# A decoder layer on one core: the last key blocks of two heads mixed together, and a few orders changed

## The reference

```python
x = x + attn(layernorm(x))                       # x: 2 x 512 x 1024
x = x + fake_quant(layernorm(x)) @ fake_quant(ctx)   # ctx: 2 x 1024 x 1024
x = x + experts(layernorm(x))
# attn: q = x@Wq (32 heads of 128), k = x@Wk and v = x@Wv (8 heads), rotary on q and k,
#   softmax(causal(q@k.T / sqrt(128))) @ v, each k and v head used by 4 q heads, then @ Wo (4096 x 1024)
# fake_quant: (clip(round(x/s + z), 0, 255) - z) * s
# experts: router of 64 experts, softmax over the top 16; z = x@A.T (512), gated by expert, @ B.T, times 2
```

## Time and profile before

| | |
|---|---|
| median of 3 runs | 1296.77 us (1296.71 to 1297.16) |
| the profiled execution | 1296.9 us, span 1295.1 us |
| mean granted clock of TensorE | 0.997 |
| TensorE busy | 1262.9 us of 6929 matmuls and transposes, 98% of the span |
| VectorE, ScalarE, GpSimd busy | 835.9 (65%), 767.2 (59%), 609.0 (47%) |
| one head unit with two jobs | about 10.3 us |
| transfers | mean 161 GB/s over the span |

### The profile page before, as it was taken

One profiled execution on the slowest core, in us unless ns is written; L12 is line 12 of the kernel. 1 busy time (PEld: TensorE's weight loads), 2 busy tenths in 40 slices (PEclk: granted clock), 3 DMA queues, 4 the chain that ended last, 5 costly groups with the idle time before them and its releaser, 6 DMA issues. The chain is left out here.

```text
span 1295.1 us, 19782 instructions
## 1 busy us (share of the span) xinstructions
PE 1262.9 (98%) x6929; PEld 1085.7 (84%) x6929; DVE 835.9 (65%) x1866; ACT 767.2 (59%) x1577; POOL 609.0 (47%) x450
## 2 busy tenths in 40 slices
PE   9999999999999999999999998999999999998998
PEld 8898998888888888888888887878888887766887
DVE  7774735556556656656556565655786788788763
ACT  4412247767777877777777877863333355565530
POOL 4777666779758777677766754420000000021100
PEclk9999999999999999999999999999999999999999
DMA  8033245558659568486485678758874486201111
GB/s 276 25 131 123 79 134 188 155 138 210 218 151 244 164 169 244 133 204 169 118 237 143 158 221 259 212 177 259 283 200 128 152 273 217 79 7 29 50 42 49
DMA packets 122403, 208.74 MB, mean 161 GB/s; under 512 B 15408, under 2 KB 56368, under 8 KB 118720
## 3 DMA queue, kind: packets, MB, share of 16 engines
q1 hardware_dynamic: 118272, 178.10, 42.5%
q0 software_dynamic: 4032, 29.36, 12.2%
HBM read 147.40 MB, written 88.08 MB: 182 GB/s over the span
## 5 line engine op out<-in xcount | busy, mean ns | idle before, releaser
L1253 DVE TENSOR_TENSOR pT_lo<-banks,pT_hi 128x512 fp32r<-128x512 f32 (+1 forms) x192 | 103.6, 595 | 170.7 <-ACT pT_hi L984 170.7
L1665 PE MATMUL banks<-ob_hi,oa_hi 128*128 128x512 f32 x384 | 149.5, 389 | 0.9 <-DVE ob_lo L1293 0.9
L1665 PE MATMUL banks<-ob_hi,oa_lo 128*128 128x512 f32 x384 | 149.4, 389 | 0.0
L1665 PE MATMUL banks<-ob_lo,oa_hi 128*128 128x512 f32 x384 | 149.4, 389 | 0.0
L1623 PE MATMUL banks<-xc,nring_hi_a 128*128 128x512 f32 x448 | 139.9, 393 | 2.1 <-DVE q_made L1203 2.1
L1623 PE MATMUL banks<-xc,nring_hi_b 128*128 128x512 f32 x448 | 139.5, 392 | 0.0
L968 ACT CAST oa_hi<-oraw 128x1024 fp32r<-128x1024 f32 x48 | 50.4, 1050 | 142.9 <-PE banks L1665 129.1
L984 ACT CAST pT_hi<-banks 128x512 fp32r<-128x512 f32 (+1 forms) x192 | 86.6, 527 | 66.0 <-PE banks L1593 66.0
L1879 POOL TENSOR_TENSOR resid<-resid,colterm 128x1024 f32<-128x1024 f32 x8 | 19.0, 2379 | 216.6 <-ACT colterm L1937 137.5
L737 POOL TENSOR_TENSOR q_lo<-q_raw,q_hi 128x512 fp32r<-128x512 f32 x64 | 87.0, 1360 | 38.5 <-ACT q_hi L921 38.2
L1578 PE MATMUL banks<-kT,q_hi 128*128 128x512 f32 (+2 forms) x384 | 104.2, 352 | 0.0
(11 more groups left out here) (256 smaller groups left out, 3413.8 us busy)
## 6 DMA issues: line engine op xcount, KB each, us to landing
q_raw<-qk_dram SPq DMA_DIRECT2D x64, 256.0 KB, 4.2
o_S<-o_st SPq DMA_DIRECT2D x64, 256.0 KB, 4.0
w<-in_L_attn_Wo SPq DMA_DIRECT2D x32, 512.0 KB, 5.9
oraw<-o_S SPq DMA_DIRECT2D x32, 512.0 KB, 3.7
nraw<-in_L_attn_Wq SPq DMA_DIRECT2D x28, 512.0 KB, 5.3
o_S<-o_S POOLq DMA_DIRECT2D x12, 1024.0 KB, 10.0
o_S<-o_N POOLq DMA_DIRECT2D x12, 1024.0 KB, 10.2
resid<-in_x SPq DMA_DIRECT2D x16, 512.0 KB, 7.1
```

The costliest lines, as they stand in the source:

```text
L1253: nc.vector.tensor_tensor(pT[1][:, sl], turned_chunk(turned, mixed, c), as32(pT[0][:, sl]), ALU.subtract).then_inc(pT_lo, 1)
L1665: ins = nc.tensor.matmul(step_bank(m, t), oa[a][:, s % 2, k, t * P:(t + 1) * P], ob[c][:, s % 2, k, :], start=(q == 0 and k == 0 and i == ...
```

## The change

1. The last key block (j = 3) of two neighbouring units, v = 2m and v + 1, is mixed together. Both have the same k and v head. `pT` grows from 1280 to 1408 columns: an even unit's transposed block 3 is put at column 512, an odd unit's at column 1024, so both are there when the odd unit is mixed. `mix` leaves block 3 out; in odd units three matmuls of 256 columns over both blocks go to `turned[:, 1, 0:256]` in bank 4.
2. VectorE adds them up (`add_pair`, three instructions): it copies the odd unit's 128 columns to SBUF and adds them to `mixed`, and adds the even unit's 128 columns, which stay in PSUM, to `o_st[0]` (subtracts them for batch 1). It runs after `normalise` of the next even unit, the last one after `step_low(0)`.
3. Those who wait for the addition (`pair_added`): ScalarE's `keep_out` of odd units, TensorE before the second chunk of the transposes of even units, and SyncE's `keep_out` of even units. SyncE now issues `keep_out(u - 3)` and `keep_out(u - 2)` together in its odd iterations. At the end `load_step(0)` and `load_step(1)` go ahead of the last two.
4. Memory: `identb` and `one` share their place with the copy of the odd block and are made by GpSimd after the last addition, not at the start; `small` shrinks, and the mask sum of tile 0 is kept in `prob`.
5. Start: 60 warm-up transposes instead of 72; the row statistics of tile 1 are made by ScalarE in five instructions (two passes over 1024 columns with sums).
6. Unit 57: the first half of step 1 (`first_high(1)`) on ScalarE goes behind the copies of the probabilities of unit 56, on GpSimd behind q's low part.
7. Last stretch: the loop's turn i = 1 is written out in another order. z of tile 0 goes before root(2) and scale_of(2), the b parts 6 and 7 before the reading of product 3, and the gate of tile 1 before product_stats(3), root(3) and scale_of(3).

```diff
-WARM = 72
+WARM = 60
-KEYS_AT = {0: 0, 1: 512, 3: 896, 2: 1024}
-CHUNKS = ((0, (0,)), (512, (1, 3)), (1024, (2,)))
+CHUNK_KEYS = ((0,), (1, 3), (2,))
+PT = 1408
+    def keys_at(u, j):
+        return {0: 0, 1: 640, 2: 1152, 3: 1024 if u % 2 else 512}[j]
+    def chunk_at(u, c):
+        return (0, 640 if u % 2 else 512, 1152)[c]
+    def last_blocks(part):
+        return pT[part][:].rearrange("p (k c) -> p k c", c=P)[:, 4:9:4, :]
...
         def keep_out(u):                                   # SyncE
             sp.wait_ge(o_copied, u + 1)
+            if u % 2 == 0:
+                sp.wait_ge(pair_added, u // 2 + 1)
...
-            if u >= 2:
+            if u >= 3 and u % 2:
+                keep_out(u - 3)
                 keep_out(u - 2)
...
-        keep_out(UNITS - 2)
         load_step(0)
         load_step(1)
+        keep_out(UNITS - 2)
         keep_out(UNITS - 1)
...
-            for f in steps_of(u + 1):                      # GpSimd
-                first_low(f)
-                if f == 0:
-                    turn_added(JOBS - 1)
+            if u == LAST_JOB_UNIT:
+                first_low(0)
+                turn_added(JOBS - 1)
+            elif u == LAST_JOB_UNIT + 1:
+                for f in range(1, 4):
+                    first_low(f)
+            else:
+                for f in steps_of(u + 1):
+                    first_low(f)
...
         def keep_out(u):                                   # ScalarE
             act.wait_ge(mix_done, u + 1)
+            if u % 2:
+                act.wait_ge(pair_added, u // 2 + 1)
             if u >= 2:
                 act.wait_ge(o_kept[u % 2], o_count(u - 2))
...
+            if u == LAST_JOB_UNIT + 1:                     # after probs_high
+                first_high(1)
...
+        def add_pair(u):                                   # VectorE
+            dve.wait_ge(o_copied, u)
+            dve.wait_ge(mix_done, u + 1)
+            link(nc.vector.tensor_copy(pair_kept, turned[:, 1, P:2 * P]))
+            nc.vector.tensor_tensor(mixed[:, H - P:H], mixed[:, H - P:H], pair_kept, ALU.add)
+            nc.vector.tensor_tensor(o_st[0][:, H - P:H], o_st[0][:, H - P:H], turned[:, 1, 0:P],
+                                    ALU.subtract if batch_of(u) else ALU.add).then_inc(pair_added, 1)
-        for t in range(TPB):
+        for t in (0, 2, 3):
             ln_stats(t)
+        dve.wait_ge(act_stats, 1)
...
             normalise(u)
+            if u > 0 and u % 2 == 0:
+                add_pair(u - 1)
...
             for c in range(3):                             # TensorE, turn_probs
+                if c == 1 and u > 0 and u % 2 == 0:
+                    pe.wait_ge(pair_added, u // 2)
...
-            for j in range(TPB):                           # TensorE, mix
+            for j in range(TPB - 1):
                 w = H - j * P
                 for p, (a, c) in enumerate(PASSES):
                     ins = nc.tensor.matmul(mixed[:, j * P:H], vv[a][:, h % 2, j, :],
-                                           pT[c][:, KEYS_AT[j]:KEYS_AT[j] + w],
-                                           start=(j == 0 and p == 0), stop=(j == TPB - 1 and p == 2))
+                                           pT[c][:, keys_at(u, j):keys_at(u, j) + w],
+                                           start=(j == 0 and p == 0), stop=(j == TPB - 2 and p == 2))
+            if u % 2:
+                for p, (a, c) in enumerate(PASSES):
+                    ins = nc.tensor.matmul(turned[:, 1, 0:2 * P], vv[a][:, h % 2, TPB - 1, :], last_blocks(c),
+                                           start=(p == 0), stop=(p == 2))
             ins.then_inc(mix_done, 1)
...
         scale_of(2)                                        # VectorE, last stretch; z of tile 0 stands before it
+        row_term(3)
         late_scale(0)
+        lows("b", range(6, 8))
+        add_product(3)
+        quantise(4)
+        gate(1)
+        add_out(0, 0)
+        lows("x", (4, 5))
+        add_out(0, 1)
+        product_stats(3)
+        scale_of(3)
+        late_stats(TPB + 2)
+        late_stats(TPB + 3)
```

More of the change, by code:

```diff
@@ L123, in build @@
         ident = sb("ident", [P, P], F32)
-        identb = sb("identb", [P, P], BF16)
+        late = sb("late", [P, 2, P], BF16)
+        identb, one = late[:, 0, :], late[:, 1, :]
+        pair_kept = late[:].rearrange("p n c -> p (n c)").bitcast(F32)
         stats = sb("stats", [P, TT, 2, 6], F32)
@@ L154, in build @@
             prob = sb2("prob", [P, 1280], F32)
-            pT = [sb2(f"pT_{n}", [P, 1280], F32R) for n in ("hi", "lo")]
-            small = sb2("small", [P, 256], F32)
+            pT = [sb2(f"pT_{n}", [P, PT], F32R) for n in ("hi", "lo")]
             n_sin = sb2("n_sin", [P, H], F32)
@@ L864, in _ @@
                 accumulate_plain(u // 8)
+        pool.wait_ge(pair_added, UNITS // 2)
+        nc.gpsimd.tensor_copy(identb, ident[:]).then_inc(ident_made, 1)
+        nc.gpsimd.memset(one, 1.0).then_inc(one_made, 1)
         pool.wait_ge(step_done, 2)
@@ L878, in _, with ln_stats @@
     def _(act):
+        link = Links(act, act_link)
+        def ln_stats(t):
+            act.wait_ge(x_in[t], 16)
+            link(nc.scalar.activation(raw[:, 0, :], resid[:, t, :], ACT.Identity, accum_out=moments[:, t, 0:1]))
+            link(nc.scalar.activation(moments[:, t, 0:1], moments[:, t, 0:1], ACT.Identity, scale=1.0 / D))
+            link(nc.scalar.activation(lnw[:, 2, t:t + 1], moments[:, t, 0:1], ACT.Identity, scale=-1.0))
+            link(nc.scalar.activation(raw[:, 0, :], resid[:, t, :], ACT.Square, bias=lnw[:, 2, t:t + 1],
+                                      accum_out=moments[:, t, 1:2]))
+            nc.scalar.activation(moments[:, t, 1:2], moments[:, t, 1:2], ACT.Identity, scale=1.0 / D
+                                 ).then_inc(act_stats, 1)
         def root(n):
@@ L983, in probs_high @@
                     act.wait_ge(mix_done, u)
-                nc.scalar.copy(pT[0][:, CHUNKS[c][0]:CHUNKS[c][0] + CHUNK_WIDTH[c]],
+                nc.scalar.copy(pT[0][:, chunk_at(u, c):chunk_at(u, c) + CHUNK_WIDTH[c]],
                                turned_chunk(turned, mixed, c)).then_inc(pT_hi, 1)
@@ L1071, in _ @@
                 keep_job(JOB_AT[u, 0])
-            if (u + 1, 1) in STEP_AT:
+            if (u + 1, 1) in STEP_AT and u > LAST_JOB_UNIT:
                 first_high(STEP_AT[u + 1, 1])
@@ L1466, in _ @@
             step_low(s)
+            if s == 0:
+                add_pair(UNITS - 1)
             if 4 <= s < 4 + PAIRS:
@@ L1589, in turn_probs @@
                 dst = turned_chunk(turned, mixed, c)
-                for j in CHUNKS[c][1]:
+                for j in CHUNK_KEYS[c]:
                     for i in range(j, TPB):
-                        col = KEYS_AT[j] - CHUNKS[c][0] + (i - j) * P
+                        col = keys_at(u, j) - chunk_at(u, c) + (i - j) * P
                         ins = nc.tensor.transpose(dst[:, col:col + P],
@@ L1978, in _ @@
         highs("x", (2, 3))
+        high("z", 0)
         root(2)
         normalise(2)
-        for i in range(1, TT):
-            if 1 < i < TT - 3:
+        highs("b", range(6, 8))
+        read_product(3)
+        scale_tile(4)
+        exponentials(1)
+        highs("x", (4, 5))
+        root(3)
+        normalise(3)
+        for i in range(2, TT):
+            if i < TT - 3:
                 scale_tile(i + 3)
@@ L1985, in _ @@
                 read_product(i + AHEAD)
-            if i == 1:
-                scale_tile(i + 3)
             high("z", i - 1)
-            if i == 1:
-                highs("b", range(6, 8))
             if i == 2:
@@ L2132, in _ @@
         product_stats(2)
+        low("z", 0)
         scale_of(2)
+        row_term(3)
         late_scale(0)
-        for i in range(1, TT):
+        lows("b", range(6, 8))
[9 more added lines that the diff above has]
+        late_stats(TPB + 3)
+        for i in range(2, TT):
             if i + AHEAD < TT:
@@ L2139, in _ @@
             low("z", i - 1)
-            if i == 1:
-                lows("b", range(6, 8))
             if i + AHEAD < TT:
```

24 lines of the change are left out of this document (10 added, 14 removed).

## The result

The changed kernel takes 1343.76 us (median of 4 runs, 1339.54 to 1347.65) against 1296.74 before, a ratio of 1.036 with a 95% interval of 1.034 to 1.038. It is slower, as forecast, but by 47 us where 17 were forecast, and outside the range. The profiled run is the longest of the four, 1347.65 us with a span of 1345.5; its parts are weighed against the profiled run of before, +50.7.

A forecast was written before the change was run, and what follows sets the result against it. TensorE, busy 98% of the span, was taken as the bound. Mix -5.5, unit 57 -1.7, experts -2.6, start -0.1, additions +1.0, stores +23 and clock +3.4 gave +17.5 on 1296.9, so 1314 us; range 1292 to 1328.

The forecast's parts named there:

- The signs named for it: ScalarE's o_st copies wait 2 to 7 us for stores in units 5, 11, 27, 45; no wait at unit 57's mix.
- Mix: TensorE's mix: -0.34 us per even unit, +0.03 per odd unit, taken as 5.5 us saved up to unit 54.
- Additions: VectorE's three additions per pair: free except 0.7 us for unit 50 and 0.3 at the last unit, sum +1.0 us.
- Stores: Even units' later stores hold ScalarE's copy and stall TensorE in nine odd units: 36.1 us worked out, +23 taken.
- The clock: Half clock on TensorE behind new gaps over 3 us: two stretches, +3.4 us; bounds 0 to 11.7.
- The rival's ground against it: Against the full queue's claim that every gap over 3 us slows the clock: gaps of 2 us left it alone.
- Unit 57: Step 1's first half moved behind unit 56's probabilities: mix(56) starts earlier, net -1.7 us, bounds -4.3 and +1.
- Last stretch: Experts, gate of tile 1 ahead of product_stats(3): fifth product starts earlier, -2.6 us; at most 5.1 gained, at least +1.
- Start: Tile 1's statistics off VectorE: -0.1 us, between -1.5 and +0.3; +1.7 if the clock falls in the warm-up gap.
- the full queue: Rival: store queue as full as now or fuller, every gap over 3 us slows the clock: +39, 1336 us; chance 0.08.

The follow-up runs named there:

- e9: Kernel before plus mixing in pairs alone, each even unit's store issued in the even iteration behind its additions; start, unit 57 and last stretch as before: 1306.17 us.
- e1: Changed kernel with one move on SyncE: in odd iterations the even unit's store is issued first of all: 1312.96 us.
- e2: Changed kernel with TensorE's gaps in units 5, 11, 21, 27, 45 and 53 filled with transposes that nobody reads: 1343.93 us.
- e4: e1 with the last stretch in the order of before on ScalarE and VectorE: 1313.55 us.
- e10: Changed kernel with even stores issued in even iterations behind the additions, but from iteration 58 on first in the odd iteration: 1301.10 us.
- f1: e13 with ScalarE's copy to o_st made 12 times instead of once in units 10, 22, 34 and 42, to make four gaps: 1319.22 us.
- f2: f1 with TensorE kept busy in the four gaps by transposes that nobody reads: 1314.39 us.
- e13: e12 with the order of unit 57 as in the change: 1291.29 us.
- e12: e9 with only units 0 to 49 mixed in pairs, from unit 50 on everything as before: 1293.11 us.
- f4: f1 with 8 copies instead of 12, so shorter gaps: 1305.00 us.
- e3: Kernel before with one edit: SyncE issues the stores of units u - 3 and u - 2 together in odd iterations, no pairs mixed: 1341.47 us.

## Why the prediction was wrong

The mechanism was right, and it alone decided; two of its sizes were wrong, and with them the time. The signs named for it came too: ScalarE's copies wait for stores of `o_st` in units 5, 11, 27 and 45, and the wait at unit 57's mix is gone.

- **Mix.** -0.34 and +0.03 were worked out, -0.35 and +0.03 measured.
- **Additions.** Unit 50: 0.7 forecast, +0.89 at the start of unit 51. Elsewhere they are free up to unit 49. At the end, 57 and on, they cost 2.9 us a pair in e9, where SyncE waits for them ahead of the steps' loads; the change puts SyncE's wait elsewhere, and there units 59 to 62 lost 0.0. The last pair was taken at 0.3: from the start of unit 63 to the last product with Wo pass 282.8 us in the change and 282.0 before, and 282.8 to 283.3 in e1, e2, e4 and e10, which mix that pair too; so it cost some 0.8.
- **Stores, the first step that failed.** The working gave 36.1 us in nine units and named the right ones: the six large gaps were 3.1, 5.9, 7.3, 5.0, 4.2 and 6.7, and measured 4.7, 6.2, 7.7, 4.4, 6.6 and 7.1 (from start to start, less the usual spacing). I then took 6 of the 17.0 us of units 13, 21 and 53, because the moved store was part of the traffic and SyncE would start earlier. Both grounds fell: in unit 53 the store alone took 12.0 us, and in e1, where SyncE issues it first, a turned product's issues still stand ahead of it in unit 21. Only unit 13 came out small (1.0 of 3.0), although its stores landed up to 13.8 us after issue. Unit 45 was 2.4 us longer than worked out, since SyncE waited before it, until 696.8 us, for the turned product of a k head to land. So 36.6 us stood in the six and 39.1 in the nine units where 23 were taken, above my upper end of 36. (One reading was off by 0.1: the last chunk stands behind eight of the ten transposes, not seven.)
- **The clock, the second.** Two stretches at 1.7 us were taken, seven came in the head units, of 3.4 to 10.2 us, 47.8 in all. They cost 13.1 us behind the six gaps. I had the gap of 3.2 us with half clock behind it in the earlier trace rows and saw that several new ones would be over 3; all six were, and f1 against f2 shows that half clock has a price. The rival's ground against it, that gaps of 2 us leave the clock alone, did not fit the gap of 1.89 us in the earlier trace rows. Six stretches at the 1.7 of the earlier trace rows would have been 10; the rest is that most were longer than the 3.4 us seen before.
- **Unit 57.** -1.7 forecast; e13 against e12 gives -1.8, within the noise. In the change unit 57 gained 2.4, but units 56 and 58 lost 2.4 and 2.0. In unit 56 it is the clock in part: the change has 3.4 us at half clock behind a gap of 1.96 us ahead of it, and the same gap before, 1.89 us long, was followed by none.

```profile
764.78 1.31 PE L1593 MATMUL banks<-ident,prob 128*128 128x128 f32 x10 [1.89 <-ACT prob L1003]
```

```profile
813.12 1.35 PE L1645 MATMUL banks<-ident,prob 128*128 128x128 f32 x10 [1.96 <-ACT prob L1035]
```

- **Last stretch.** -2.6 forecast. From its first product with ctx to the end pass 157.1 us in the change and 158.0 before, but the ten other kernels with the old order take 156.2 to 157.4, so no gain is shown. The gate of tile 1 ahead of the sum does shorten the waits: the fifth product begins 3.6 us earlier after the first than it did, more than forecast. VectorE is then late for the sixth by 4.2 us, with half clock behind, the sixth is only 1.1 us earlier, and the eighth 0.6 later. I had followed VectorE's queue only to the fifth.
- **Start.** -0.1 forecast, +0.6 at unit 0; but the profiles with the old start reach unit 0 between 0.1 us earlier and 1.1 later than that of before, so this is open. TensorE's gap ahead of the first fills is 3.0 us. The clock falls there in five of the nine profiles with the new start and in none of the nine with the old, and these five reach unit 0 1.0 to 1.2 us later than before: the 1.7 that I had left outside the sum is a real case.

Of the rivals the full queue (1336) was nearest, with a chance of 0.08; it had the mechanism of both misses. The page "DMA: Bandwidth & Descriptors" of the Trainium skill (Anatomy of one DMA) would have made the stalls an estimated 12 us. The rows after don't bear it out as a forecast: where it gives an estimated 2.6 us for 256 KB, the stores of this run took 2.0 to 13.8, the middle one 3.6, and that of unit 53 12.0. The fit is given there for GpSimd's path, and these stores go by SyncE's; the row of the same place before was the better guide (12.2 in unit 53, 3.5 to 4.0 in unit 5).

## What to carry to other kernels

A saving on the bound engine is cheap to work out; what decides is which buffer now stays full for longer, and who must empty it before whom. When a store or load moves to another place of an in-order queue, take the landing time that the trace shows at that place, at full size, and do not reduce it without a row that shows why. Price every gap of TensorE of 3 us or more with the half clock behind it, here 1.3 to 2.6 us each, and count on it behind more than one in three of those from 1.5 to 3 us. And leave a saving out of the stretches in which other engines are late: with pairs only up to unit 49, and the start and last stretch as before, 1301 became 1291 (e10 and e13), though which of the three gave how much is only shown for the pairs, by e9 against e12.

## What the runs showed of the hardware

In the head units half clock follows the gap and not the matmuls: in f1 four gaps of 4.2 to 5.9 us brought four stretches of 3.4 or 6.8 us, in f2 the same four waits, filled with transposes to within some 1.1 us, none. Gaps near 2 us go either way: those of f4 brought none, one of 1.96 us in the changed kernel (813.12 us) and the one of 1.89 in the earlier trace rows did. Over the eighteen profiles, all 37 gaps of TensorE of 3 us or more (the start of the kernel left out) were followed by half clock (it begins in the gap or within 2 us behind it), 44 of the 116 from 1.5 to 3 us, and none of the 60 from 1.0 to 1.5. The clock can also fall without such a gap: in e10 at 1152.0 us and in e4 at 1166.7, in the same part of the last stretch, with no idle time over 0.5 us in the 8 us before; what brought it there is open.

A store of 256 KB landed between 2.0 and 13.8 us after its issue in one and the same run. That this is what makes the changed kernel vary by 8 us over four runs is not shown: e3, which waits for such stores as well, varied by 3.4, and e10, which hardly does, by 8.4 over twelve.
